# Decoder-attention kernel: unit 8 joins the units whose cache pages are read directly, and the transposing transfers take over from unit 9 instead of unit 10

## What is computed

```python
w = weight[adapter_ids]                       # layer 0: one 512x512 adapter for each sequence
x = x + einsum('bsi,boi->bso', x, w)
# layer 1: paged attention, 32 query heads of 128, 8 key/value heads, cache of 512 keys + 128 new ones
q, k, v = x @ Wq.T, x @ Wk.T, x @ Wv.T        # q and k: RMS norm, then rotary embedding
kc = k_cache[block_table]                     # 16 pages of 32 keys for each sequence
scores = q @ concat(kc, k).T * SCALE          # masked beyond the cached length
x = x + (softmax(scores) @ concat(vc, v)) @ Wo.T
```

## Time and profile before

| | |
|---|---|
| median of 3 runs | 1010.57 us (1010.1 to 1010.78) |
| the profiled execution | 1009.46 us, of which the span of its instructions is 1007.7 us |
| TensorE busy | 995.9 us, 99% of the span |
| VectorE, ScalarE, GpSimd busy | 85%, 80%, 78% |
| DMA engines, mean busy share | 80 to 90% in most of the 40 slices |
| granted TensorE clock | 1.0 throughout |

### The profile page before, as it was taken

How to read it: one execution, slowest core, us unless ns; L and a number is a source line. 1 busy time by engine, 2 the same in 40 slices (tenths; PEclk the granted TensorE clock), 3 DMA queues, 4 the chain that set the end, 5 groups by cost and what they waited for, 6 DMA issues and landing times.

```text
span 1007.7 us, 19405 instructions
## 1 busy us (share of the span) xinstructions
PE 995.9 (99%) x5511; PEld 866.5 (86%) x5511; DVE 859.8 (85%) x1784; ACT 805.3 (80%) x2101; POOL 788.0 (78%) x805
## 2 busy tenths in 40 slices
PE   8999999999999999999999999999999999999998
PEld 5778888988888888888888888888888888888887
DVE  7776667679999899999998999899999999998985
ACT  4555556678889889888988898898889888988884
POOL 3886777547889879897898888898798978888672
PEclk9999999999999999999999999999999999999999
DMA  8999889889888898888888888798888888897873
GB/s 259 275 255 268 257 201 264 227 196 187 159 159 161 159 160 156 163 156 152 172 155 158 160 165 159 147 166 152 173 148 165 155 154 163 154 172 146 151 148 85
DMA packets 502858, 177.92 MB, mean 177 GB/s; under 512 B 419025, under 2 KB 484962, under 8 KB 502754
## 3 DMA queue, kind: packets, MB, share of 16 engines
q1 hardware_dynamic: 379552, 145.56, 70.2%
q10 hardware_dynamic: 122178, 29.03, 13.6%
q0 software_dynamic: 1024, 2.10, 0.9%
HBM read 105.06 MB, written 31.47 MB: 135 GB/s over the span
## 4 chain that ended last, share of the span: by engine, by line
PE 96%; DVE 1%; ACTq 1%; issue 1%; ACT 0%; POOL 0%; DVEq 0%; POOLq 0%
PE S L1388 22%; PE O L1321 7%; PE O L1323 7%; PE O L1322 7%; PE Q L1321 6%; PE Q L1323 6%; PE Y L1321 6%; PE Q L1322 6%; PE Y L1323 6%; PE Y L1322 6%; PE T L1327 5%; PE KV L1322 3%; PE KV L1321 3%; PE KV L1323 3%; PE KV L1341 1%
## 5 line engine op out<-in xcount | busy, mean ns | idle before, releaser
L1062 DVE SCALAR_TENSOR_TENSOR pr<-pr,rc,raw 128x640 f16<-128x640 f32 x212 | 247.9, 1169 | 15.5 <-ACT raw L803 8.5
L1034 DVE CUSTOM_DVE_ANT_0 pr<-S,mask,rst 128x640 f32<-128x640 f32 x256 | 225.5, 881 | 18.3 <-PE S L1388 15.5
L823 ACT ACTIVATE pr<-pr,nb 128x640 f32<-128x640 f32 x256 | 211.7, 827 | 17.6 <-DVE nb L1034 17.5
L803 ACT ACTIVATE raw<-pr,rc 128x640 f16<-128x640 f32 x212 | 169.8, 826 | 1.2 <-DVE rc L1050 0.9
L603 POOL TENSOR_TENSOR m<-m 128x512 f32<-128x512 f32 x63 | 111.4, 1767 | 74.6 <-DVE m L1101 69.8
L556 POOL TENSOR_TENSOR kl<-raw,kh 128x512 fp32r<-128x512 f32 x64 | 97.0, 1515 | 41.5 <-ACT kh L706 40.4
L1388 PE MATMUL S<-kh,qh 128*128 128x320 f32 x512 | 120.7, 317 | 3.8 <-DVE nb L1034 3.7
L577 POOL TENSOR_SCALAR ptl<-first 128x512 fp32r<-128x512 f16 x135 | 107.6, 797 | 17.2 <-issue 6.0
L1388 PE MATMUL S<-kh,ql 128*128 128x320 f32 x512 | 116.6, 309 | 0.0
L1388 PE MATMUL S<-kl,qh 128*128 128x320 f32 x512 | 116.1, 308 | 0.3 <-POOL kl L556 0.3
L769 ACT ACTIVATE Q<-Q 128x128 f32<-128x128 f32 x256 | 68.3, 267 | 56.5 <-DVE m L1101 56.4
(11 more groups left out here) (177 smaller groups left out, 2693.9 us busy)
## 6 DMA issues: line engine op xcount, KB each, us to landing
wraw<-in_wall SPq DMA_DIRECT2D x74, 256.0 KB, 4.5
raw<-cache_rows SPq DMA_DIRECT2D x61, 256.0 KB, 3.8
cache_rows<-in_kv SPq DMA_DIRECT2D x68, 224.0 KB, 4.3
cache_rows<-in_kv ACTq DMA_DIRECT2D x60, 224.0 KB, 5.3
raw<-cache_rows ACTq DMA_DIRECT2D x51, 256.0 KB, 4.9
mask<-mask_rows SPq DMA_DIRECT2D x64, 128.0 KB, 4.0
first<-in_lw SPq DMA_DIRECT2D x5, 1024.0 KB, 7.2
acc<-in_x SPq DMA_DIRECT2D x8, 256.0 KB, 7.5
```

What stands on the lines that cost most here:

```text
L803: e.activation(upper16[:, g, :], pr[:, slot(u, g), :], ACT.Copy, scale=rc[:, u % 2, g:g + 1]).then_inc(a_f1, 1)
L823: e.activation(pr[:, slot(u, g), :], pr[:, slot(u, g), :], ACT.Exp, bias=nb[:, u % 2, g:g + 1], scale=-1.0, accum_out=sm[:, u % 2, g:g + 1 ...
L1034: e.tensor_tensor_reduce(pr[:, slot(u, g), :].rearrange("p (a n) -> p a n", a=2), S[:, :, 0:320], mask[:, u % 2, :].rearrange("p (a n) -> ...
L1062: e.scalar_tensor_tensor(out=lower16(u, g), in0=pr[:, slot(u, g), :], scalar=rc[:, u % 2, g:g + 1], in1=upper16[:, g, :], op0=ALU.mult, op ...
```

## The change

The first unit turned by DMA becomes 9 instead of 10, and the units read directly become nine (0 to 8) instead of eight. Unit 8 is head 1 of sequence 0, so its pages are rows 2 and 3 of the cache. `load_kt` gets the row `2 * hk + 1`, and the gathers get a second table of row numbers, which lies in the place of the page table `tabb` and is made by one small VectorE instruction in period 2 (`key_rows_1`). Head 1 of sequence 0 need not be copied any more: the pages of sequence 0 are copied last and with 12 rows instead of 14. Since units 9 to 15 are now the first users of the copy, the order of the sequences is 1, 2, ..., 7, 0. The groups are spread otherwise over the periods. The buffers that go by `u % 2` now go by `place(u) = (u - NA) % 2`, which mirrors them.

```diff
-NL = NB
-NA = 10
+NL = NB + 1
+NA = 9
...
-COPY_SP = (0, 1, 1, 1, 1, 1, 2, 3, 3, 3, 0, 1, 0)
-COPY_ACT = (2, 2, 2, 2, 2, 2, 2, 1, 0, 0, 0, 0, 0)
+COPY_SP = (0, 1, 1, 1, 1, 1, 1, 2, 3, 0, 1, 1, 1, 1)
+COPY_ACT = (2, 2, 2, 2, 2, 2, 2, 2, 1, 0, 0, 0, 0, 0)
...
-    return [divmod(k, NGRP) for k in range(first, first + (COPY_ACT if act else COPY_SP)[period])]
+    return [((k // NGRP + NL) % NB, k % NGRP)
+            for k in range(first, first + (COPY_ACT if act else COPY_SP)[period])]
...
+        kidx1 = tabb[:, 0:NT * (NL - NB)]
...
+        def place(u):
+
+            return (u - NA) % 2
+
         def slot(u, g):
 
-            return (u % 2) * G + g if u < NA else (G * (u - NA) + g) % RING
+            return G * place(u) + g if u < NA else (G * (u - NA) + g) % RING
...
         def load_kt(e, regs, v, t):
             if v >= 2 and t == 0:
                 e.wait_ge(g_kc, v - 1)
-            first_page = NPG * v + 4 * t
+            hk, b = divmod(v, NB)
+            first_page = NPG * b + 4 * t
...
                 e.dma_start(
-                    rawk[v % 2][:, k * PSZ:(k + 1) * PSZ],
-                    kv[1, bass.ds(numbers[j], 1), :].rearrange("a (p n) -> (a p) n", p=P)
+                    rawk[raw_at(v)][:, k * PSZ:(k + 1) * PSZ],
+                    kv[2 * hk + 1, bass.ds(numbers[j], 1), :].rearrange("a (p n) -> (a p) n", p=P)
                 ).then_inc(d_rawk[v % 2], 16)
...
         def copy_page(e, b, k, number):
 
-            e.dma_start(copy[2:, b, k, :].rearrange("r (s n) -> s r n", s=16),
-                        kv[2:, bass.ds(number, 1), :].rearrange("r a (s n) -> (a s) r n", s=16)
+            rows = slice(2 if b >= NL - NB else 4, 2 * NK)
+            e.dma_start(copy[rows, b, k, :].rearrange("r (s n) -> s r n", s=16),
+                        kv[rows, bass.ds(number, 1), :].rearrange("r a (s n) -> (a s) r n", s=16)
                         ).then_inc(d_copy[b], 16)
...
             def gather_v(v, t):
+                hk, b = divmod(v, NB)
                 if t == 0:
                     e.wait_ge(c_kidx, 1)
+                    if hk == 1:
+                        e.wait_ge(c_kidx1, 1)
                     if v >= 2:
                         e.wait_ge(g_vlo, v - 1)
+                rows_of = (kidx, kidx1)[hk]
...
+            def key_rows_1():
+                e.tensor_scalar(kidx1, tabf[:, 0:NT * (NL - NB)], 32.0, rowsb[:, 2:3], ALU.mult, ALU.add
+                                ).then_inc(c_kidx1, 1)
```

More of the change, by code:

```diff
@@ L168, in build @@
         qw_s, kw_s = qkw_s[:, 0:D], qkw_s[:, D:2 * D]
-        ang = pr[:, 0, 0:512].rearrange("p (b f) -> p b f", b=NB)
-        rnd = pr[:, 1, 0:512].rearrange("p (b f) -> p b f", b=NB)
+        ang = pr[:, G * (NA % 2), 0:512].rearrange("p (b f) -> p b f", b=NB)
+        rnd = pr[:, G * (NA % 2) + 1, 0:512].rearrange("p (b f) -> p b f", b=NB)
         sn = acc[:, NB - 2, :].rearrange("p (b f) -> p b f", b=NB)
@@ L175, in build @@
         lws = first[:, HID:5 * HID].rearrange("p (t n) -> p t n", t=4)
-        upper = pr[:, G:2 * G, :].rearrange("p g k -> p (g k)")
+        upper = pr[:, G - G * (NA % 2):2 * G - G * (NA % 2), :].rearrange("p g k -> p (g k)")
         lws1 = upper[:, 0:2048].rearrange("p (t n) -> p t n", t=4)
@@ L202, in plane_tile @@
         def plane_tile(u, which, t):
-            return planes[u % 2][which].rearrange("p (g t) n -> p g t n", g=G)[:, :, t, :]
+            return planes[place(u)][which].rearrange("p (g t) n -> p g t n", g=G)[:, :, t, :]
         S = pb("S", [P, 2, 512])
@@ L232, in build @@
                                                sem("c_mask_new"))
-        c_ilf, c_tabf, c_kidx, c_pos, c_ang, c_sin, c_cos = (
-            sem("c_ilf"), sem("c_tabf"), sem("c_kidx"), sem("c_pos"), sem("c_ang"), sem("c_sin"),
+        c_ilf, c_tabf, c_kidx, c_kidx1, c_pos, c_ang, c_sin, c_cos = (
+            sem("c_ilf"), sem("c_tabf"), sem("c_kidx"), sem("c_kidx1"), sem("c_pos"), sem("c_ang"), sem("c_sin"),
             sem("c_cos"))
@@ L306, in raw_at @@
         def raw_at(u):
-            return u % 2 if u < NA else 0
+            return place(u) if u < NA else 0
         def taken(u):
@@ L448, in turn_upper @@
                 e.dma_start_transpose(
-                    planes[u % 2][0][:, 10 * pair:10 * pair + 10, :],
+                    planes[place(u)][0][:, 10 * pair:10 * pair + 10, :],
                     upper16[:, 2 * pair:2 * pair + 2, :].rearrange("p g k -> p (g k)")
@@ L460, in turn_lower @@
                 e.dma_start_transpose(
-                    planes[u % 2][1][:, 10 * pair:10 * pair + 10, :],
+                    planes[place(u)][1][:, 10 * pair:10 * pair + 10, :],
                     pr[:, slot(u, 2 * pair), :].bitcast(F16)
@@ L543, in gather_v @@
             def gather_v(v, t):
+                hk, b = divmod(v, NB)
                 if t == 0:
                     e.wait_ge(c_kidx, 1)
+                    if hk == 1:
+                        e.wait_ge(c_kidx1, 1)
                     if v >= 2:
                         e.wait_ge(g_vlo, v - 1)
+                rows_of = (kidx, kidx1)[hk]
                 e.indirect_dma_start(
-                    out=rawv[v % 2][:, t, :], out_offset=None,
+                    out=rawv[raw_at(v)][:, t, :], out_offset=None,
                     in_=kv.rearrange("c a (r d) -> (c a r) d", d=D),
                     in_offset=bass.IndirectOffsetOnAxis(
-                        ap=kidx[:, NT * v + t:NT * v + t + 1], axis=0)
+                        ap=rows_of[:, NT * b + t:NT * b + t + 1], axis=0)
                 ).then_inc(d_rawv[v % 2], 16)
@@ L1021, in largest @@
                     if h % 2 == 0:
-                        e.wait_ge(d_t2[h // G % 2][h % G // 2], taken(NA + h // G))
+                        e.wait_ge(d_t2[(NA + h // G) % 2][h % G // 2], taken(NA + h // G))
                     else:
@@ L1195, in _ @@
                 turn = w >= 0
+                if i == 2:
+                    key_rows_1()
                 if o >= 0:
@@ L1649 @@
     p = np.arange(P)
-    consts = np.concatenate([np.stack([p, p % 32, p], axis=1), np.broadcast_to(inv, (P, 64))],
+    consts = np.concatenate([np.stack([p, p % 32, p % 32 + 2 * 64 * PSZ], axis=1), np.broadcast_to(inv, (P, 64))],
                             axis=1).astype(np.float32)
```

## The result

The changed kernel took **1005.44 us** as the median of 5 executions (1005.11 to 1006.1), the kernel before 1010.57 us (1010.1 to 1010.88): ratio 0.995, 95% interval 0.9936 to 0.9965, 5.1 us less. Eleven further executions, measured later beside 16 of the kernel before, gave something else: median 1008.55 us against 1010.1 (ratio 0.999, 0.9979 to 1.0002). The granted clock was 1.0 in both profiled executions; in later executions of these two kernels it lay between 0.997 and 1.0, so the "full speed throughout" at the top holds for the executions behind the forecast and not for all that follow.

A forecast was written before the change was run, and what follows sets the result against it. TensorE, busy 995.9 of 1007.7 us, was taken to bound the kernel. Terms -2.2 + 0 + 0 + 0 = -2.2 us, against the median 1010.57, gave 1008.4 us; 8-in-10 range 1007.5 to 1010.3.

The forecast's parts named there:

- A period of the first kind becomes one of the second: -2.20 us: TensorE, period 10: unit 9's 20 probability transposes go, so 16.72 us becomes 14.52; 2.0 us kept as other end.
- The switch keeps its wait of 0.67 us: TensorE's wait behind the switch stays, one period earlier; a rival that it goes too gave 1007.7 us, chance 0.05.
- Switch, weights: cost 0, or 0.2: Two weight chunks' splits on ScalarE and GpSimd meet the first planes, covered by waits: 0, or 0.2 us if cover fails.
- Unit 8's page loads, `key_rows_1`, gathers: 0: SyncE, VectorE and GpSimd, periods 6 to 8: reading unit 8 directly costs 0; bad end 1.6 us, gathers rival chance 0.14.
- limit given: 162: Sign of being right on the gathers: GpSimd's values of unit 7 start before 162 us.
- the forecast's own sign of being wrong: TensorE idle behind GpSimd's `m`, the query sum, would show the forecast wrong.
- The eight additional page copies of ScalarE: 0: ScalarE only issues them and has over 6 us of idle time a period, so they cost 0.
- Copies in periods 10 to 13: 0: Copy groups beside transposing transfers fit idle DMA time: 0, far end 0.4 us a period; rivals 1010.0 (0.13), 1016.5 (0.07).
- How the numbers follow: Forecast's own range 1007.9 to 1009.0 us, with 0.3 us for run spread; chances faster 0.48, same 0.45, slower 0.07.

The follow-up runs named there:

- a nudge of 3: Changed kernel with 3 identity transposes put ahead of TensorE's turning of the queries for unit 14: median 1006.41 us; the same in the kernel before: 1008.43 us.
- the nudges 1 and 3: Both kernels with 1 identity transpose ahead of TensorE's query turning for unit 14 and 3 for unit 18: 1006.34 us changed, 1007.84 us before.
- the split moved: Changed kernel with 1 and 3 extra transposes for units 14 and 18, and GpSimd's weight split in period 9 put ahead of the keys' lower half: 1005.39 us.

## Where the forecast was right, and which steps failed

*A period of the first kind becomes one of the second: -2.20 us.* Right. The mark-to-mark times around the switch fell by 1.7 us, which is 2.2 less the new gap of 0.51; without the gap they fell by 2.2.

*The switch keeps its wait of 0.67 us.* Right: 0.67.

*Switch, weights: cost 0, or 0.2.* Wrong: 0.51 us. The step looked at the splits on their own engines, where GpSimd had 4.36 us of idle time ahead of the next keys, and not at what stands beside them: VectorE's `lower_plane` of the first transferred unit. The page of the kernel before had a sign, since this instruction took 1.17 us on average there and 0.88 us at the switch. The Trainium skill (SBUF — State Buffer, Who interferes with whom) says that a VectorE instruction with two SBUF inputs contends with a GpSimd instruction that reads SBUF, and calls their shared ports an exclusive lock. If the second simply waited for the first, the price would be, as an estimate from the rows of before, 0.76 us: the split would run from 220.79, where the keys end, to 222.09, and `lower_plane` starts at 221.33. The trace agrees in kind; the measured 0.51 us decides.

*Unit 8's page loads, `key_rows_1`, gathers: 0.* Right in the profiled execution, and not in every one. Values of unit 7 started at 161.32 (limit given: 162), and the query sum had 1.1 us of slack where the forecast had 0.85. In period 8 the forecast had 3 us free; the profiled execution had 1.9, and in the one with a nudge of 3 (a later place, which can't act on period 8) it was used up, which is the forecast's own sign of being wrong:

```profile
182.64 0.63 POOL L603 TENSOR_SCALAR vh<-raw 128x512 fp32r<-128x512 f32 x1 [4.42 <-DMA raw<-in_kv,tabb]
...
185.94 0.66 PE L1348 MATMUL T<-ident,m 128*128 128x128 f32 x4 [0.28 <-POOL m L618]
```

The kernel before has the same kind of wait in period 7 in one of its traces (0.5 us), so it is a tail of both kernels and not the change's alone.

*The eight additional page copies of ScalarE: 0.* Right in six traces of seven; in the seventh one such issue took 3.27 us, and TensorE waited 1.1 us.

*Copies in periods 10 to 13: 0.* Right: from there on TensorE has no idle time, and `ptl` waits for no DMA. But it rests on the table: with three groups in the period of the switch the kernel was 9 us slower than before.

*The step that failed for the number* is in "How the numbers follow": the forecast took the spread of the three executions, 0.3 us, for the spread of the kernel, and took the 14.52 us of the earlier trace rows for a constant of the code. In fact the 50 steady periods take 14.46 or 14.52 us, 3.0 us in all, by which of two stable rhythms an execution falls into. All executions of before behind the forecast, and the two more of that measurement, were at the high value by their times (and the profiled one by its periods), all five of the changed kernel at the low one; so some 3 of the 5.1 us were this. No run shows a cause for that draw, so it counts as chance: the next eleven of the changed kernel gave 1008.55 us, next to the forecast's 1008.4, and that would have been luck as well, since the gap of 0.51 us and its tail were not in the sum. At equal values the change is worth 1.0 to 2.1 us, most directly 1.5 (the nudges 1 and 3) and 1.7 (the trace). With the split moved it is 2.2 by the trace, as forecast.

*Open:* what in TensorE, or between it and the others, makes the two rhythms; and whether the change alters how often each comes. 7 of 16 against 24 of 100 looks like it, but the 7 are 5 of 5 on one occasion and 2 of 11 on the next. The kernel before, too, had 0 of 5, 2 of 19, 5 of 16, 12 of 34 and 5 of 25 on its occasions. These were not all on the same chip, and no run separates the chip from the rest.

## What to carry to other kernels

A loop bound by one engine that is never idle can still have two speeds: before a fraction of a per cent is put down to an edit, look at the list of times for two groups and at one periodic instruction for the length of the period, and compare kernels at the same value, which nudges of a few tenths of a microsecond could set here. When a change moves a boundary in the program against a fixed table, look at what runs beside each instruction at the new place on the other engines, not only at the idle time of its own. And a transfer that is hidden is hidden by the table that spreads it: the same table of copies with the switch one period earlier made the kernel 9 us slower here.

## What the runs showed of the hardware that I had not expected

TensorE's matmuls of 512 columns (granted clock 1.0, no idle time) do not all follow each other at the same distance: in the product with the values it was 0.230 us in periods of 14.52 us and 0.227 in periods of 14.46, in one kernel and one execution. A delay of 0.11 us moved a steady period of 14.46 us to 14.52 in both kernels, one of 0.32 us (3 transposes) moved it back, with the same outcome of each of the first four nudges in either. VectorE's plane instruction with float16 output takes 0.88 us beside an idle GpSimd and 1.39 where it started 0.6 us into a subtraction of 128x512 there, which had 0.7 us left. SyncE took 9.66 us to issue 12 page copies of 224 KB in the run with the switch at 9 and unit 8 copied; the first transposing transfer behind them was issued at 217.47 us, against 206.56 in the changed kernel. One page copy took ScalarE 3.27 us to issue in one execution, and the one just before it 0.56 us.
